# Two y1 copies moved ahead on ScalarE in the first step of layer 2, and halved layer-one rows in its last step

## The reference

```python
x = _layernorm(x + _L0_gnn_ref(x, adj, ...))           # aggregate, two dense layers, batch norms
x = _layernorm(x + _L1_gnn_ref(x, ..., adj, src, dst)) # attention over 256 edges, then W_out
x = _layernorm(x + _L2_gnn_ref(x, adj, adj, W1, W2, W3))
x = _layernorm(x + _L3_gnn_ref(x, adj, W, a))          # dense attention over neighbours

def _L2_gnn_ref(x, adj, S, W1, W2, W3):
    def _slconv(x, adj, S, W):
        support = jnp.einsum('bnf,fh->bnh', x, W)
        return jnp.einsum('nm,bmh->bnh', adj * S, support)
    h = jax.nn.relu(_slconv(x, adj, S, W1))   # 128 -> 256
    h = jax.nn.relu(_slconv(h, adj, S, W2))   # 256 -> 512
    return _slconv(h, adj, S, W3)             # 512 -> 128
```

## Time and profile before

| what | before |
|---|---|
| median of three runs | 552.51 us (551.27 to 552.89) |
| the profiled execution: time | 550.63 us |
| its span, from the first to the last instruction | 548.9 us |
| TensorE busy | 526.6 us, 96% of the span |
| ScalarE busy | 371.9 us, 68% |
| VectorE busy | 415.2 us, 76% |
| GpSimd busy | 203.4 us, 37% |
| chain that ended last, by engine | PE 83%, DVE 11%, POOL 2%, ACT 2% |

### The profile page before, as it was taken

The page is one execution under the profiler, slowest core; times in us unless marked ns, Lnnn a source line. Parts: engine busy times, 40 slices in busy tenths (PEclk is TensorE's granted clock), DMA queues, the critical chain, the costliest instruction groups (busy, mean ns, idle before and its releaser), DMA issues.

```text
span 548.9 us, 11011 instructions
## 1 busy us (share of the span) xinstructions
PE 526.6 (96%) x3516; PEld 463.3 (84%) x3516; DVE 415.2 (76%) x1465; ACT 371.9 (68%) x752; POOL 203.4 (37%) x245
## 2 busy tenths in 40 slices
PE   7999998999999899999999999999999999999964
PEld 6998535688888889989989989989999998989953
DVE  5899677998686463588696786787687776679796
ACT  4776794777656544366787686795785787686773
POOL 4970352257674305027136037027126016110213
PEclk9999999999999999999999999999999999999987
DMA  6631000222100000000001000000100100100002
GB/s 191 188 95 41 0 0 20 72 75 66 39 0 1 2 1 1 1 1 1 1 2 41 0 1 17 21 0 0 38 0 0 38 1 1 38 2 1 21 19 77
DMA packets 28419, 15.29 MB, mean 28 GB/s; under 512 B 2353, under 2 KB 28081, under 8 KB 28385
## 3 DMA queue, kind: packets, MB, share of 16 engines
q1 hardware_dynamic: 27536, 13.38, 8.5%
q0 software_dynamic: 560, 1.25, 0.8%
q10 hardware_dynamic: 288, 0.26, 0.2%
HBM read 10.69 MB, written 4.19 MB: 27 GB/s over the span
## 4 chain that ended last, share of the span: by engine, by line
PE 83%; DVE 11%; POOL 2%; ACT 2%; issue 1%; POOLq 0%; DVEq 0%
PE psum L293 15%; PE psum L295 15%; PE psum L294 15%; PE psum L2135 10%; PE psum L1934 5%; PE psum L1982 3%; PE psum L2077 3%; PE psum L2087 3%; PE psum L1993 2%; PE psum L2181 2%; PE psum L1997 2%; PE psum L2163 2%; PE psum L2006 2%; DVE soft L1087 1%; PE psum L2155 1%
## 5 line engine op out<-in xcount | busy, mean ns | idle before, releaser
L209 POOL TENSOR_TENSOR ln_r<-ln_v,mhalf 128x8 f32<-128x8 f32 x25 | 41.7, 1666 | 203.6 <-DVE ln_v L203 203.6
L2135 PE MATMUL psum<-l2w_s,h 128*128 128x128 f32 x512 | 59.7, 275 | 0.0
L2135 PEld LDWEIGHTS psum<-l2w_s,h 128*128 128x128 f32 x512 | 59.0, 192 | 0.6
L293 PE MATMUL psum<-qt_hi,l2w_s_hi 128*128 128x512 f32 x128 | 52.8, 413 | 0.0
L295 PE MATMUL psum<-qt_hi,l2w_s_lo 128*128 128x512 f32 x128 | 50.7, 396 | 0.0
L294 PE MATMUL psum<-qt_lo,l2w_s_hi 128*128 128x512 f32 x128 | 50.6, 395 | 0.0
L287 ACT ACTIVATE keep_x<-keep_x,ln_b,ln_r (+1 forms) x104 | 42.7, 486 | 2.6 <-POOL ln_b L212 2.6
L1664 ACT ACTIVATE h<-psum 128x512 f32<-128x512 f32 x60 | 34.8, 594 | 11.7 <-PE psum L295 11.6
L293 PE MATMUL psum<-wgt_hi,h_hi 128*128 128x256 f32 x128 | 37.1, 290 | 0.9 <-DVE h_lo L1064 0.9
L295 PE MATMUL psum<-wgt_hi,h_lo 128*128 128x256 f32 x128 | 35.8, 279 | 0.0
L294 PE MATMUL psum<-wgt_lo,h_hi 128*128 128x256 f32 x128 | 35.7, 279 | 0.0
(11 more groups left out here) (297 smaller groups left out, 1748.7 us busy)
## 6 DMA issues: line engine op xcount, KB each, us to landing
keep_x<-in_x SPq DMA_DIRECT2D x32, 128.0 KB, 3.0
xin<-in_x SPq DMA_DIRECT2D x32, 128.0 KB, 2.2
out_x<-ob SPq DMA_DIRECT2D x24, 128.0 KB, 1.8
out_x<-keep_x SPq DMA_DIRECT2D x8, 128.0 KB, 2.0
l2w_raw<-in_l2w POOLq DMA_DIRECT2D x1, 512.0 KB, 4.8
adjs<-in_adj_t ACTq DMA_DIRECT2D x2, 128.0 KB, 2.7
adjs<-in_adj SPq DMA_DIRECT2D x2, 128.0 KB, 3.0
l2w_s<-in_l2w POOLq DMA_DIRECT2D x1, 256.0 KB, 4.8
```

What stands on the lines that cost most here:

```text
L209: pool.tensor_tensor(ln.r[:].rearrange("p s k -> p (s k)"), ln.v[:].rearrange("p s k -> p (s k)"), mhalf[:], ALU.pow).then_inc(ln.root, 1)
L293: pe.matmul(o, lhs[0], rhs[0], start=start, stop=False)
L2135: i = pe.matmul(bank(s)[:, 0, k * D:(k + 1) * D], h2[:, s, g, j * N + t * P:j * N + (t + 1) * P], l2w3_s[:, g, :], start=(g == 0), stop=(g ...
```

## The change

In step 0 both `y1_turned` copies are issued ahead of the two `pt_high` copies on ScalarE, where before each stood ahead of its slot's `h1_high`. In step 7, slot 0, the layer-one rows go graph by graph: `hidden1` signals after each graph's six multiplications, ScalarE and VectorE copy each graph's bank by itself (128x512 each, where one instruction took both banks, 128x1024), and `mix_hidden` starts when the first graph's low part is there, and waits for the second ahead of its own multiplications of graph 1. The counts of the signals that follow go up by one.

```diff
 # VectorE
+            def h1_low(p, s, more=0):
+                dve.wait_ge(h1_hi, 2 * p + s + 1 + more)
...
             for s in range(2):
-                h1_low(L, s)
+                if s == 0:
+                    for j in range(2):
+                        dve.wait_ge(h1_hi, 2 * L + j + 1)
+                        dve.scalar_tensor_tensor(out=h1[1][:, 0, j].rearrange("p t f -> p (t f)"), in0=bank(j)[:, 0, :], scalar=0.0,
+                                                 in1=h1[0][:, 0, j].rearrange("p t f -> p (t f)"),
+                                                 op0=ALU.max, op1=ALU.subtract).then_inc(h1_lo, 1)
+                else:
+                    h1_low(L, 1, 1)
 # ScalarE
             def step(p, two_ahead=True, ahead=True, behind=True, two_behind=True, first=False):

+                if first:
+                    for s in range(2):
+                        y1_turned(p + 1, s, 6 - 4 * s)
                 for s in range(2):
                     pt_high(p, s)
                 for s in range(2):
-                    if ahead:
-                        y1_turned(p + 1, s, 2 if s and first else 6 + s)
+                    if ahead and not first:
+                        y1_turned(p + 1, s, 6 + s)
                     h1_high(p, s)
...
-            for s in range(2):
-                h1_high(L, s)
+            for j in range(2):
+                act.wait_ge(h1_done, 2 * L + j + 1)
+                act.activation(h1[0][:, 0, j].rearrange("p t f -> p (t f)"), bank(j)[:, 0, :], ACT.Relu).then_inc(h1_hi, 1)
+            h1_high(L, 1, 1)
 # TensorE
-            def hidden1(p, s):
+            def hidden1(p, s, halves=False):

                 pe.wait_ge(pt_lo, 2 * p + s + 1)
                 for j in range(2):
+                    if halves and j:
+                        i.then_inc(h1_done, 1)
...
-            def mix_hidden(p, s):
-
-                pe.wait_ge(h1_lo, 2 * p + s + 1)
+            def mix_hidden(p, s, halves=False, more=0):
+
+                pe.wait_ge(h1_lo, 2 * p + s + 1 + more)
                 for f in range(GA):
                     for j in range(2):
+                        if halves and f == 0 and j:
+                            pe.wait_ge(h1_lo, 2 * p + s + 2)
...
-                hidden1(L, s)
-            for s in range(2):
-                mix_hidden(L, s)
+                hidden1(L, s, halves=s == 0)
+            for s in range(2):
+                mix_hidden(L, s, halves=s == 0, more=s)
```

More of the change, by code:

```diff
@@ L1060, in pt_low @@
                 dve.tensor_tensor(pt[1][:, s, :], bank(4 + s)[:, 0, :], pt[0][:, s, :], ALU.subtract).then_inc(pt_lo, 1)
-            def h1_low(p, s):
-                dve.wait_ge(h1_hi, 2 * p + s + 1)
+            def h1_low(p, s, more=0):
+                dve.wait_ge(h1_hi, 2 * p + s + 1 + more)
                 dve.scalar_tensor_tensor(out=h1[1][:, s].rearrange("p j t f -> p (j t f)"),
@@ L1651, in pt_high, with h1_high @@
                 act.activation(pt[0][:, s, :], bank(4 + s)[:, 0, :], ACT.Copy).then_inc(pt_hi, 1)
-            def h1_high(p, s):
-                act.wait_ge(h1_done, 2 * p + s + 1)
+            def h1_high(p, s, more=0):
+                act.wait_ge(h1_done, 2 * p + s + 1 + more)
                 act.activation(h1[0][:, s].rearrange("p j t f -> p (j t f)"), bank(2 * s, 2).rearrange("p k c -> p (k c)"),
```

## The result

The changed kernel takes 548.66 us in the median of 5 runs (548.07 to 549.30), beside 551.81 us for the kernel before in the same comparison (5 runs, 551.27 to 552.89): a ratio of 0.9949, with an interval of 0.9933 to 0.9964. The profiled execution took 548.14 us with a span of 546.4, which is 2.5 us less than that of before (548.9).

The account below looks back on a forecast made before the run. TensorE, busy 96% of the span, was taken as the bound. Step 0's 1.48 us and step 7's 0.30 make 1.78 us less, from the median 552.51 to 550.7 us, range 549.4 to 552.4.

Parts of the forecast that it names:

- Step 0, 1.48 us: Layer 2's first step: TensorE's 1.6 us wait for `y1t` goes, `mix_hidden` starts at 190.00 instead of 191.50; gain 1.48 us.
- the 0.37 us that were to come for `h_lo`: Step 0, ahead of slot 0's `mix_hidden`: a new TensorE wait of 0.37 us for VectorE's low part, already taken off the gain.
- the slower rival: Step 0: the early copies block ScalarE if `attend1` of slot 1 ends past 186 us; 554.3 us at 5 us delay; chance 0.04.
- Step 7, 0.30 us: Last step: the halves remove the `h_lo` wait, 0.98 us, but TensorE reaches the transposes only 0.30 us earlier.
- The wait of 0.6 us for `qt_lo`: Step 7, ahead of the transposes: a new TensorE wait of some 0.6 us for slot 0's `qt_lo`, made behind `ln_v`.
- the cover: Step 7: VectorE has 0.6 us between the second half's end at 482.86 and its next start at 483.49.
- 0.33 of 0.98 us: Step 7: 0.98 us is the whole `h_lo` wait, won entirely in the rival where both waits go whole (550.0 us, chance 0.10).
- Behind 489 us I let all of it through: After step 7's transposes: the whole gain reaches the end, TensorE having no wait of note to the sum of 519.75.
- the range's low end: 549.4 us, given as the both-waits-whole case (550.0 us) less half of the earlier runs' 1.6 us spread.

Follow-up runs that it names:

- the repeat: The changed kernel run again unaltered beside the kernel before: 548.16 us (9 runs, mean 548.57), ratio 0.9958.
- both kernels of before with added multiplications: The kernel before plus ten or five unread multiplications of constants in TensorE's 2.5 us wait near the end: 550.19 us with ten, 550.17 with five.
- the delayed one: The changed kernel with the first multiplication of the last step's `mix_hidden` (slot 0) made 19 times more: 550.32 us, ratio 0.9991.
- With five, the kernel before: The kernel before plus five unread multiplications of constants in TensorE's 2.5 us wait near the end: 550.17 us, ratio 0.9981.
- the changed kernel with five: The changed kernel plus five unread multiplications of constants in TensorE's 2.5 us wait near the end: 548.86 us, ratio 0.9959.
- the ten: Ten unread multiplications of constants in TensorE's 2.5 us wait near the end: added to the changed kernel 548.12 us, to the kernel before 550.19.

## Why the prediction was right, and where it was wrong

The forecast was 550.7 us, with 549.4 to 552.4 around it, and it took 548.66. Both terms of the sum were right; what stands behind them was not.

*Step 0, 1.48 us: right.* Measured 1.50. The list of waits has no entry for the 0.37 us that were to come for `h_lo`, since the modelled end of the multiplication before it leaves a gap of 0.12 us (188.70 plus 1.05 to 189.87). The wait is there all the same: from the eight short multiplications to `mix_hidden` TensorE takes 1.17 us (188.70 to 189.87), where it took 0.81 before (to 191.50):

```profile
190.69 1.06 PE L2087 MATMUL psum<-wot,y1t 128*128 128x128 f32 x8
```

VectorE's row says for what:

```profile
188.59 2.59 DVE L1064 SCALAR_TENSOR_TENSOR h_lo<-psum,h_hi 128x1024 fp32r<-128x1024 f32 x2 [1.94 <-ACT h_hi L1662]
```

The first of the two ends 1.23 us behind 188.59, at 189.82, and `mix_hidden` starts at 189.87, 0.05 us behind it, as reckoned. ScalarE's new order made nothing late, so the slower rival didn't come.

*Step 7, 0.30 us: right.* In step 7 itself it is 0.33 (9.80 or 9.81 us against 9.47 or 9.48). The second column gives 0.27 over the five profiles with halves (297.28 to 297.57, mean 297.39) and the five without (297.58 to 297.75, mean 297.66), with the loop's 0.3 us of drift in it. The wait of 0.6 us for `qt_lo` came as forecast, and moving `qt_lo` showed that it was the holder. The halves were cheaper than I took them, 1.28 us for both where I had 1.38, which changed nothing, since the cover was there. By the Trainium skill (Perfetto Trace Analysis, section Optimizing Scalar/DVE Operations) an access of VectorE to PSUM costs about 125 ns; the second one cost 0.05 us here (1.28 less 1.23), so the measurement decides. The same section's advice to break instructions up paid 0.33 of 0.98 us, because what TensorE needs next, `qt_lo`, comes from a chain on VectorE that the halves did not bring forward.

*"Behind 489 us I let all of it through": this is the step that failed.* The sum took over the end of the profiled execution as it was, on the ground that TensorE goes on without a wait of note and that the others are released by it. But in that execution the chain of the end ran over TensorE from 531.54 to 537.57, up to 537.00 at half clock, and VectorE waited 0.9 us for it. TensorE's list also has a wait of 0.9 us for `soft` behind 519 us that the prediction leaves out. All of this was there in the chain, the list of waits and the clock column, and the sum uses nothing behind 519.75 us. The changed kernel's execution had no such wait of VectorE, and its end was 0.84 us shorter. The forecast put that term at nothing and had no case in which the end becomes shorter. Nor does the range's low end follow from its own rule: 550.0 less half of 1.6 is 549.2 and not 549.4; 548.66 lies below either.

*The miss in parts.* From 550.73 (552.51 less 1.78) to 548.66 it is 2.07 us. 0.70 is the median of before, which was 551.81 in the comparison and not 552.51. The other 1.37 is the difference between 3.15 and 1.78. Of it 0.8 to 1.0 is the wait at the end where it goes away, as the third column has it; what is left, 0.4 to 0.6, is not shown to be more than the spread of the runs, since the repeat gave 2.5 in the mean. That the wait goes in most runs of the changed kernel and stays in most of the one before is what the times suggest; the profiles show it in two of two and two of two. Why the changed kernel has the shorter stretch at half clock is not shown.

## What to carry to other kernels

A wait that goes is worth the distance to the next thing that is late on the same engine, and that is found by taking each instruction queued behind it and asking when its operand is there without the edit. Read the chain to its very end, with the granted clock beside it: a bound that TensorE sets only because it stands at half clock can go in a version whose edits lie elsewhere, and so be in the time and not in the sum. To size a change that is smaller than the spread of the times, compare distances between fixed rows close around the edit inside each trace; here they repeat within 0.01 us around an edit and 0.3 us over the loop, where the runs spread over 3.

## What the hardware showed that I had not expected

A low-clock stretch also came in the middle of the kernel, in three profiles of fourteen (both kernels of before with added multiplications, and the delayed one), ahead of every edit in them. In the 2 us before it TensorE idled for no more than 0.22 us, and the profiles without the fall have the same rows there. With five, the kernel before has there

```profile
164.00:166.00 2.00, 2.00 (x8) 1.48 (x8) 0.69 (x1) 0.95 (x3) 2.00 (x3) 0.50 0.00 0
```

and the changed kernel with five

```profile
164.00:166.00 2.00, 2.00 (x12) 1.45 (x11) 0.69 (x1) 1.09 (x3) 2.00 (x4) 1.00 0.00 0
```

TensorE is the bound there, and the way to the same multiplication is 1.65 us longer (129.87 us from TensorE's 206th instruction to its 836th, against 128.2 in the other eleven). At the end, where VectorE is the bound, a stretch of the same length cost nothing (third column 56.06 with it, 56.05 with the ten and without it). The same clock has a price in one place and none in another.

The added f32 multiplications of constants with 256 columns are recorded as two each, 0.22 us apart (2.32 us for ten records), where the kernel's split ones of the same shape start every 0.12 us.
